# A graph diffusion followed by a mixture of experts: three PSUM banks and six row buffers for the experts' results, a contiguous row for the planes, other places for a table, for weaved matmuls and for the combination

## What is computed

```python
x = x + gnn(layernorm(x))
x = x + ffn(layernorm(x))

def gnn(h):                                   # W_in, W_out: 256 x 256
    h = silu(h @ W_in.T + b_in)
    out = term = h
    for i in range(1, 7):                     # K_STEPS = 6, GAMMA = 0
        term = segment_sum(term[src], dst) / degree[:, None] / i
        out = out + term
    return out @ W_out.T + b_out

def ffn(x):                                   # E = 8 experts, 2 for each row, H = 512
    xn = layernorm(x) * gamma + beta
    w = softmax(top_k(xn @ Wr + br, 2))
    return sum(w_e * (gelu(xn @ W1[e] + b1[e]) @ W2[e] + b2[e]) for the two e of each row)
```

## Time and profile before

| what | us |
|---|---|
| three timed runs | 1213.09, 1216.51, 1216.91 (median 1216.51) |
| the profiled execution | 1212.99 |
| its span, first to last instruction | 1211.2 |
| TensorE busy | 1150.2 (95%) |
| VectorE busy | 702.9 (58%) |
| ScalarE busy | 418.2 (35%) |
| GpSimd busy | 227.8 (19%) |

### The profile page before, as it was taken

The page is one execution under the profiler, slowest core; times in us unless marked ns, Lnnn a source line. Parts: engine busy times, 40 slices in busy tenths (PEclk is TensorE's granted clock), DMA queues, the critical chain, the costliest instruction groups (busy, mean ns, idle before and its releaser), DMA issues.

```text
span 1211.2 us, 26287 instructions
## 1 busy us (share of the span) xinstructions
PE 1150.2 (95%) x7856; PEld 816.0 (67%) x7856; DVE 702.9 (58%) x1425; ACT 418.2 (35%) x806; POOL 227.8 (19%) x278
## 2 busy tenths in 40 slices
PE   5798999999999999999999999999999998999993
PEld 3686766766566666666666666666666666889993
DVE  7898999994444433443155424443254677776566
ACT  1566655663100000000022101211022236777682
POOL 2000000000011121111100000000022237567752
PEclk8998999999999999999999999999999999999998
DMA  6111011013334424443334313331224333223476
GB/s 159 55 43 39 27 31 30 25 34 102 86 92 93 90 57 110 95 102 64 69 107 130 99 43 97 107 102 52 37 90 128 111 113 91 88 80 94 124 212 190
DMA packets 77196, 105.98 MB, mean 87 GB/s; under 512 B 13559, under 2 KB 62510, under 8 KB 76988
## 3 DMA queue, kind: packets, MB, share of 16 engines
q1 hardware_dynamic: 63997, 75.26, 21.0%
q0 software_dynamic: 11376, 25.55, 9.4%
q10 hardware_dynamic: 1740, 4.11, 1.3%
HBM read 77.00 MB, written 37.49 MB: 95 GB/s over the span
## 4 chain that ended last, share of the span: by engine, by line
PE 78%; DVE 10%; DMA 4%; issue 3%; ACT 2%; DVEq 2%; POOL 1%; ACTq 0%; SPq 0%; POOLq 0%
PE ps L2000 45%; PE ps L2054 8%; PE ps L1978 7%; PE ps L1946 5%; PE ps L2168 4%; PE ps L2182 4%; DVE v_b L1239 4%; PE ps L1914 1%; DMA h_ring<-h_dram 1%; PE ps L1925 1%; DVE adj L1146 1%; DMA adj<-xs_dram,v_a 1%; PE ps L2082 1%; ACT v_b L1084 1%; POOL y_dram L855 0%
## 5 line engine op out<-in xcount | busy, mean ns | idle before, releaser
L2000 PE MATMUL ps<-v_a,adj 125*125 125x512 f16 x1375 | 297.3, 380 | 0.0
L2000 PE MATMUL ps<-v_b,adj 125*125 125x512 f16 x1250 | 270.2, 380 | 1.7 <-DVE v_b L1264 1.7
L2000 PEld LDWEIGHTS ps<-v_a,adj 125*125 (+1 forms) x1375 | 188.2, 137 | 108.3
L2000 PEld LDWEIGHTS ps<-v_b,adj 125*125 x1250 | 171.1, 137 | 100.5 <-issue 2.1
L959 ACT ACTIVATE t_hi<-ps,cinv 125x256 f32<-125x256 f32 x125 | 59.1, 473 | 454.9 <-PE ps L2000 396.6
L1246 DVE SCALAR_TENSOR_TENSOR t_hi<-ps,cinv,t_hi 125x256 f32<-125x256 f32 x125 | 60.3, 483 | 235.7 <-ACT t_hi L959 235.7
L1239 DVE TENSOR_TENSOR v_b<-v_b 125x2560 f16<-125x2560 f16 x125 | 180.3, 1488 | 6.1 <-PE ps L1946 5.5
L2054 PE MATMUL ps<-v_b,adj 125*125 125x512 f16 x625 | 139.8, 381 | 0.2 <-issue 0.2
L934 ACT ACTIVATE adj<-ps 125x625 f32 (+1 forms) x125 | 112.1, 906 | 65.7 <-PE ps L1946 64.8
L1978 PE MATMUL ps<-v_a,adj 125*125 125x512 f16 x500 | 122.8, 379 | 0.0
L2182 PE MATMUL ps<-adj,v_b 128*128 x672 | 110.0, 275 | 10.2 <-issue 8.5
(11 more groups left out here) (279 smaller groups left out, 992.2 us busy)
## 6 DMA issues: line engine op xcount, KB each, us to landing
h_ring<-h_dram SPq DMA_DIRECT2D x125, 125.0 KB
v_a<-L_ffn_W SPq DMA_DIRECT2D x32, 256.0 KB, 3.5
v_b<-L_ffn_W SPq DMA_DIRECT2D x32, 256.0 KB, 3.5
adj<-w_dram SPq DMA_DIRECT2D x16, 512.0 KB, 5.3
adj<-y_dram SPq DMA_DIRECT2D x8, 560.0 KB
w_dram<-w_hi SPq DMA_DIRECT2D x32, 128.0 KB, 1.9
hx_dram<-h_dram POOLq DMA_DIRECT2D x25, 125.0 KB, 2.4
hx_dram<-x POOLq DMA_DIRECT2D x25, 125.0 KB, 3.2
```

The lines of the kernel that those rows point to most:

```text
L2000: last = te.matmul(ps[0:NP, u, :], of_tile(adj[0:NP, 0:ADJ], i, u, a * NP, NP), source[:, a, :], start=(a == 0), stop=(a == T - 1))
```

## The change

1. Windows: at w = 0 of a row, the tile's 25 matmuls are put behind windows 1, 2, 3, 4 as 7, 6, 6, 6, before behind windows 2, 3, 4 as 8, 8, 9. For that the tile before is taken up behind window u = 1 there, by ScalarE and by VectorE.
2. Planes: `one_plane` takes its tile numbers from a new row `tile_row16` of 56 contiguous 16-bit numbers, made by one more iota on GpSimd.
3. Banks: results rotate over the PSUM banks 4, 5 and 6; TensorE's result(j) waits for the eviction of j - 3, before j - 2. `positions` of the second tables moves to bank 7.
4. Row buffers: six instead of four; eviction j waits for scatter j - 6, before j - 4. The waits for landed scatters count six semaphores.
5. `experts_of` of the second tables is made at j = 17, before at 14, and so behind `rows_of` (15).
6. The lots 0 to 2 are combined at j = 45 to 56, four iterations a lot, with 3, 2, 3, 2 steps; before at 45 to 53 with 3, 3, 4.

```diff
+    FY = 6
+    YB = 3
...
-    assert CLASS_TILES[-1] == FT and LOT_AT + 9 < FT
+    assert CLASS_TILES[-1] == FT and LOT_AT + 12 <= FT + LAG
...
+        tile_row16 = fa(FT, F16)
...
-        y_sb = [over(adj, at_y + r * D * 4, D, F32) for r in range(FR)]
+        y_sb = [over(adj, at_y + r * D * 4, D, F32) for r in range(FY - 1)] + [fc(D, F32)]
...
-            return 16 * len(range(r, tiles, FR))
+            return 16 * len(range(r, tiles, FY))
...
+            g.iota(tile_row16, [[1, FT]], base=0, channel_multiplier=0, allow_small_or_imprecise_dtypes=True)
...
-                r = j % FR
+                r = j % FY
                 pool.wait_ge(S["y_ok"], j + 1)
...
-                        if has_early and u == EARLY_AT:
+                        if has_early and u == (1 if w == 0 else EARLY_AT):
                             early_high(r - 1 + (w - 1) // WIN, (w - 1) % WIN)
...
-                            if u == EARLY_AT:
+                            if u == (1 if w == 0 else EARLY_AT):
                                 early(r - 1 + (w - 1) // WIN, (w - 1) % WIN)
...
-                v.tensor_tensor(by_p, iota_xc[:, first:first + count, 0:1].rearrange("p y o -> p o y").broadcast_to([NP, CB, count]),
+                v.tensor_tensor(by_p, tile_row16[0:NP, None, first:first + count].broadcast_to([NP, CB, count]),
...
-                if j == 14:
+                if j == 17:
                     experts_of(FB, ends_b, FA)
                 if j == 15:
                     dve.wait_ge(S["tok_ps"], 2)
-                    rows_of(ps[:, 6, 0:PB], FA, FB)
+                    rows_of(ps[:, 7, 0:PB], FA, FB)
...
-                if LOT_AT <= j < LOT_AT + 9:
-                    n, third = (j - LOT_AT) // 3, (j - LOT_AT) % 3
-                    weighted(n, *((0, 3), (3, 6), (6, 10))[third])
+                if LOT_AT <= j < LOT_AT + 12:
+                    n, piece = (j - LOT_AT) // 4, (j - LOT_AT) % 4
+                    weighted(n, *((0, 3), (3, 5), (5, 8), (8, 10))[piece])
...
-                need(dve, y_out[j % FR], 16 * (j // FR))
-                v.scalar_tensor_tensor(y_sb[u % FR], ps[:, 4 + r, 0:D], g2[:, bass.ds(e, 1)], b2_part(bass.ds(part, 1)),
+                need(dve, y_out[j % FY], 16 * (j // FY))
+                v.scalar_tensor_tensor(y_sb[j % FY], ps[:, 4 + j % YB, 0:D], g2[:, bass.ds(e, 1)], b2_part(bass.ds(part, 1)),
...
-                        parts = (0, 0, 0, 8, 16, T) if w == 0 else (0, 5, 10, 15, 20, T)
+                        parts = (0, 0, 7, 13, 19, T) if w == 0 else (0, 5, 10, 15, 20, T)
...
-                    last = positions(6, 0, planes_b, oh_pos_b, groups, groups[0] == 0, ends, GA)
+                    last = positions(7, 0, planes_b, oh_pos_b, groups, groups[0] == 0, ends, GA)
...
-                    need(pe, S["y_ok"], j - 1)
+                    need(pe, S["y_ok"], j - YB + 1)
...
-                    last = te.matmul(ps[:, 4 + r, 0:D], hp[u % FR][:, b, :],
+                    last = te.matmul(ps[:, 4 + j % YB, 0:D], hp[u % FR][:, b, :],
```

7 lines of the change are left out of this document (4 added, 3 removed).

## The result

The changed kernel takes 1207.64 us (median of 7 runs, 1203.60 to 1208.86), the kernel before 1214.13 (7 runs, 1212.22 to 1216.91) beside it: ratio 0.9935, 95% interval 0.9915 to 0.9954, 6.5 us less. The profiled execution took 1203.97 (span 1202.2) where that of before took 1212.99, which is 9.0 us less. The two numbers differ because the runs of the changed kernel lie at two levels: three at 1203.6 to 1204.0, with a mean granted clock of 0.987, four at 1207.6 to 1208.9, with 0.982 to 0.984. The profiled one is of the first.

What follows compares the result with a forecast made beforehand. TensorE, busy 95% of the span, was taken as the bound, so only its waits and the end count. Terms -3.0 - 0.1 - 4.8 - 1.7 = -9.6 us from a four-run mean of 1214.9 gave 1205.3, predicted 1205.0; range 1199 to 1211.5.

Steps and rivals of the forecast that it cites:

- A: Whole kernel: the forecast itself, all four parts gain as summed, -9.6 us, predicted 1205.0; chance 0.55.
- B: Expert tiles: TensorE waits for hs_ok instead of y_ok, Part 3 gains only 1.5; -6.3 us, 1208.6; chance 0.15.
- C: Tail: worth nothing, combination steps and out-stores eat it; -7.9 and up to 1 us lost, 1208; chance 0.09.
- Part 2: Planes from a contiguous row: -0.25 us for each large plane; -0.1 us before the experts, the rest in Part 3.
- Part 4: Tail: six row buffers, three banks and twelve-tile combination remove waits, last scatter starts earlier; -1.7 us.
- Part 1: Windows of each row's first tile: matmuls put behind window 1 already; -0.7 us in three rows, -0.9 in row 1, total -3.0.
- Part 3: First expert tiles: three banks remove bank waits, two new waits of about 2 us, expert table moved later; -4.8 us.
- The clock: Expert iteration 6: if its 2.0 us wait halves the clock, it takes 5.7 instead of 2.9 us; 0.6 reach VectorE.
- E: Expert tiles: short waits keep TensorE at 1.2 GHz from iteration 6, 2.7 us a tile; +9.3 us, 1224; chance 0.05.
- F: Expert tiles: L2182 waits for address loads, not the bank; only Part 1 and Part 4 stay, -4.7, 1210; chance 0.07.
- D: Whole kernel: VectorE gives nothing back in Part 1 and all bank waits vanish; -14 us, 1201; chance 0.09.

Runs made afterwards that it cites:

- experiment 1: Kernel before with only the window shares of w = 0 changed; 1240.26 us against 1241.71 for the kernel before, ratio 0.9992.
- experiment 5: The changed kernel itself, run and profiled again; 1209.87 us against 1213.27 for the kernel before, ratio 0.9964.
- experiment 12: Changed kernel with expert choice spread, positions a tile later, two combination pieces behind the loop; 1242.21 us against 1247.81 for the kernel before.
- experiment 4: Changed kernel with the lots combined over nine tiles instead of twelve; 1241.64 us against 1241.71 for the kernel before, ratio 1.0007.
- Experiment 7: Changed kernel with four row buffers instead of six; 1206.48 us, ratio to the kernel before 0.9940.
- experiment 3: Changed kernel with two PSUM banks for results instead of three; 1240.05 us against 1241.71 for the kernel before, ratio 0.9988.
- experiment 11: Changed kernel with two PSUM banks for results, a second time; 1239.33 us against 1241.9 for the kernel before, ratio 0.9983.
- experiment 8: Changed kernel with planes compared against the strided row again; 1209.71 us against 1209.87 for the changed kernel.

## Why the prediction was right, point by point

The median came 2.6 us above the predicted 1205.0, and the forecast (A) describes the profiled execution: -9.6 us against -9.0. For the runs as a whole it says too much: their medians differ by 6.5 us, and 1207.64 lies nearer to what rivals B (1208.6) and C (1208) gave than to A's 1205.0. Two of the four terms (parts 2 and 4) were off in size.

**Part 1** was forecast at -3.0. The profiles differ by 2.80, of which 0.3 is there at the first window already (90.61 and 90.28); 2.5 remain, and the executions of experiment 1 together give 2.4. The replay's 9.2 us measured 9.33: window 2 still waits 0.21 us. Its 0.7 us a row measured 0.6 in rows 3 and 4 but only 0.27 in row 2, and its 0.9 in row 1 measured 0.82; in experiment 5, where the half clock lasts into these windows, row 1 gains nothing.

**Part 2**: 768 to 519 ns, as said. Its -0.1 at the start of the experts came out as -0.61, but the second profile of the same program has only -0.17 (694.14 to 693.97), with a wait of 1.12 us for the weights in front; with the planes undone the stretch is longer by 1.5 us, but that is there already at the transposes before the wait, and an execution with the new planes (experiment 12) has it too. What the first table's planes bring lies within what such a stretch varies by.

**Part 3** has the right sum by a mechanism that carries a third of it. From the first expert matmul to iteration 22 it is -4.54, forecast -4.8. The two new waits, forecast at 2.0 and 2.1 us, measured 1.72 and 1.95; the positions wait for the plane, 1.64 us; the wait behind the expert table is 0.78, not 0.2. These four are 6.09 us. Before, the five bank waits of the stretch were 3.57, 0.95, 1.17, 0.74 and 1.09, 7.52 in sum. So only **1.4 us of waiting** went. The other large piece is the half clock of before from 1027 to 1032: 38 matmuls in 5 us where 72 would go, 5 x (1 - 38/72) = 2.4 us. The second profile separates the two: with the same waits but half clock again, 3.3 us of it, the stretch takes 77.79 us, only 1.3 less than before. Rival B, the wait that only changes its name, therefore held for 6.1 of 7.5 us, and the replay, which set times of the old trace beside new ones, never asked how much of the old time was clock. VectorE's waits for the cast don't go either, 0.77 and 0.89 us remain at 1035.06 and 1040.34.

**The clock is the step that failed.** The prediction asked what a 2.0 us wait would do, gave 0.6 us, and put it "in the range". In 9 of the 12 runs of the changed kernel the mean clock is 0.980 to 0.984, and the profile of one of them pays 3.3 us. The 0.6 rested on iteration 6 at half clock with VectorE as the bound of iteration 7; in the trace the half clock comes behind the wait of iteration 7 and again around 1040, where nothing hides it. Rival E was right in kind and wrong in size and length: the clock doesn't stay down from tile to tile, and it costs 3.3 us and not 19. Its rule in the Trainium skill (TensorE: Matmul & The Clock Gate, section "A second HAM failure mode: psum-queue depth-cycling") says that going through PSUM banks in a cycle with small idle gaps can make the clock swing. A swing is in the second profile, 0.51, 1.00, 0.50 within ten microseconds; but the number of banks doesn't decide it: with two the clock falls as well, and with three it is 1.00 from 1081 to 1171. The 2.7 us a tile that E counts would be 2.5 by the rows it names (5 x 40/38 - 5 x 40/72), and what the clock takes before step 1, 1.6 us between the two profiles, was in no term.

**Part 4** was wrong: forecast -1.7, measured -0.07. Each step came: no wait for the scatter, none of TensorE for its bank; TensorE's last group starts 1.57 us earlier against iteration 53 (13.15 to 11.58). Two things took it back. The combination, spread over the last tiles, stands before the evictions: the replay had counted its steps, and put the last scatter 1.45 us behind the last eviction's start; it starts 2.4 us behind the pair's start at 1184.61. And the replay ended at the last scatter: it took the landing behind it as fixed, while the last load's issue comes 2.23 us behind the last scatter's issue where the DMA engines are idle by then, and up to 3.87 in these executions (5.13 in experiment 4) where they are not. That term was not in the sum. Experiment 7 against before shows the two sides: the combination over twelve tiles and the other edits cost 1.0 us up to the load, the six buffers win about 1.0.

**The rivals.** F fell: the banks are what L2182 waited for (experiments 3 and 11). D fell, since VectorE's waits took the place of the banks'. C, "the tail is worth nothing", is true as to the tail. The 0.92 us between iterations 22 and 53 was in no part; the second profile has 0.26 of it, so it varies by itself, with a wait for a gather of 0.35 to 0.49 us at 1152 to 1156 in some executions (before, experiments 5 and 8).

That the sum came within 0.6 us of the profiled execution is partly luck. It was right with errors on both sides: -1.6 too much in the tail, 1.4 too little in the stretches to the experts and between iterations 22 and 53, and a clock that some executions give and others don't. The five later runs, with a median of 1209.87, all lie at the second level.
